# Expert layers of a four-stage transformer stack: routing tables and token map moved into the last shared-expert tiles, first routed block written apart

## The reference, cut to what matters

```python
scores = jax.nn.sigmoid(x @ gate_w.T) + bias
topk_w, topk_idx = jax.lax.top_k(scores, TOPK)          # TOPK = 4 of E = 16 experts
topk_w = topk_w / (jnp.sum(topk_w, axis=-1, keepdims=True) + 1e-20)
cw = jnp.sum(jax.nn.one_hot(topk_idx, E, dtype=x.dtype) * topk_w[..., None], axis=1)
g = jnp.einsum('th,eih->eti', x, Wg)
u = jnp.einsum('th,eih->eti', x, Wu)
z = jax.nn.silu(g) * u
zw = z * cw.T[:, :, None]
out = jnp.einsum('eti,ehi->th', zw, Wd)
out = out + jax.nn.silu(x @ Sg.T) * (x @ Su.T) @ Sd.T   # the shared expert
```

## Time and profile before

| | |
|---|---|
| median of 3 runs | 1276.3 us (1275.05 to 1277.97) |
| the profiled execution | 1276.3 us, span 1274.5 us |
| expert layer 1, first stage ends, routed blocks start | about 71 us, 84 us of the span |
| expert layer 2, the same | about 786 us, 797 us of the span |
| TensorE, VectorE, ScalarE, GpSimd busy | 86%, 71%, 55%, 44% of the span |
| mean granted TensorE clock | 0.924 of 2.4 GHz |

### The profile page before, as it was taken

The page is one execution under the profiler, slowest core; times in us unless marked ns, Lnnn a source line. Parts: engine busy times, 40 slices in busy tenths (PEclk is TensorE's granted clock), DMA queues, the critical chain, the costliest instruction groups (busy, mean ns, idle before and its releaser), DMA issues. The chain is left out here.

```text
span 1274.5 us, 21579 instructions
## 1 busy us (share of the span) xinstructions
PE 1097.4 (86%) x5654; PEld 717.9 (56%) x5655; DVE 905.9 (71%) x1775; ACT 704.8 (55%) x1218; POOL 566.7 (44%) x582
## 2 busy tenths in 40 slices
PE   4969999999194899999997787999999947878597
PEld 3847777777182233333333675677777735467454
DVE  5869888887575888888860666888888847444632
ACT  3238787887143177777775131787888824424142
POOL 4335666664556244443331225566666545140200
PEclk9979999999596599999998888999999977989889
DMA  9367899764615550000000183789995561000001
GB/s 351 114 220 185 218 243 286 174 114 60 192 50 155 104 99 19 1 1 1 1 1 1 63 309 111 236 196 258 275 222 103 83 156 67 1 1 1 0 1 66
DMA packets 62798, 151.01 MB, mean 118 GB/s; under 512 B 12224, under 2 KB 17024, under 8 KB 58240
## 3 DMA queue, kind: packets, MB, share of 16 engines
q1 hardware_dynamic: 37440, 95.17, 22.3%
q0 software_dynamic: 22592, 50.27, 20.3%
q10 hardware_dynamic: 2688, 4.65, 1.1%
HBM read 104.89 MB, written 44.97 MB: 118 GB/s over the span
## 5 line engine op out<-in xcount | busy, mean ns | idle before, releaser
L811 POOL DMA_INDIRECT moe_acc_rows<-xn,moe_token_of x94 | 208.0, 2213 | 146.3 <-ACT xn L886 131.1
L923 DVE TENSOR_TENSOR moe_w_lo<-moe_raw,moe_w_hi 128x1536 fp32r<-128x1536 f32 x94 | 165.4, 1759 | 62.9 <-ACT moe_w_hi L874 62.7
L1977 ACT ACTIVATE causal_prob<-causal_sc 128x512 f32<-128x512 f32 (+3 forms) x384 | 166.8, 492 | 70.3 <-PE causal_sc L1882 69.7
L874 ACT CAST moe_w_hi<-moe_raw 128x1536 fp32r x94 | 138.7, 1475 | 78.0 <-issue 76.4
L1864 PE MATMUL causal_mx<-ks,causal_qs 96*128 (+4 forms) x384 | 131.4, 353 | 23.0 <-DMA causal_qs<-causal_parts 16.5
L831 PE MATMUL moe_gu<-moe_w_hi,xt_hi 128*128 128x512 f32 x282 | 148.4, 526 | 0.6 <-DVE moe_w_lo L923 0.6
L1882 PE MATMUL causal_sc<-causal_qs,ks 99*128 (+3 forms) x384 | 120.2, 333 | 1.9 <-ACT causal_prob L1977 1.7
L831 PE MATMUL moe_gu<-moe_w_hi,xt_lo 128*128 128x512 f32 x282 | 111.8, 396 | 0.0
L831 PE MATMUL moe_gu<-moe_w_lo,xt_hi 128*128 128x512 f32 x282 | 110.9, 393 | 0.0
L826 PE MATMUL moe_gu<-moe_raw,xn 128*128 x188 | 98.0, 603 | 5.0 <-ACT moe_w_hi L874 5.0
L1808 POOL TENSOR_SCALAR_AFFINE_SELECT causal_prob<-causal_prob 128x512 f32<-128x512 f32 x64 | 40.9, 639 | 115.9 <-ACT causal_prob L1977 115.5
(11 more groups left out here) (317 smaller groups left out, 2724.5 us busy)
## 6 DMA issues: line engine op xcount, KB each, us to landing
moe_raw<-in_w_gu SPq DMA_DIRECT2D x34, 1024.0 KB, 6.1
moe_raw<-in_w_down SPq DMA_DIRECT2D x34, 512.0 KB, 8.2
causal_qs<-causal_parts SPq DMA_DIRECT2D x45, 128.0 KB, 3.6
moe_acc_rows<-moe_zeros SPq DMA_DIRECT2D x2, 2304.0 KB, 14.7
moe_acc_rows<-x SPq DMA_DIRECT2D x18, 256.0 KB, 2.0
moe_xn_rows<-xn SPq DMA_DIRECT2D x2, 2048.0 KB, 10.7
x<-moe_acc_rows SPq DMA_DIRECT2D x16, 256.0 KB, 6.8
xn<-moe_acc_rows ACTq DMA_DIRECT2D x16, 256.0 KB, 7.2
```

Source lines behind the costliest of these rows:

```text
L811: pool.indirect_dma_start(acc_rows[a], bass.IndirectOffsetOnAxis(ap=token_of[:, b - 3:b - 2].bitcast(U32), axis=0), out_rows[(b - 3) % OUT ...
L874: nc.scalar.copy(w_hi[1 - s][:, :, :], raw[:, bass.ds(at + SPLIT_AT, GU_COLS - SPLIT_AT)].rearrange("p (k n) -> p k n", k=SPLIT)).then_inc ...
L923: nc.vector.tensor_tensor(w_lo[1 - s][:, :, :], raw[:, bass.ds(at + SPLIT_AT, GU_COLS - SPLIT_AT)].rearrange("p (k n) -> p k n", k=SPLIT), ...
L1977: nc.scalar.activation(prob[u % 2][:, h, o:CH], sc[(u * QPK + h) % BANKS][:, o:CH], ACT.Exp, scale=SCALE).then_inc(exp_done, 1)
```

## The change

First stage. `place()` moves on TensorE from after `down(6)` to before `turn_z(6)`, right behind `gate_up(7)`. GpSimd marks two tiles instead of three (POOL_TILES = 2) and `mark_places` six instead of five. On VectorE `tables()` is cut in three: `begin_tables` (first_of, begun, expert_f) after `add(4)`; `map_tokens` after `z_of(7)`; `place_experts` (expert_of, begun_at) after `zt_lo_of(6)`; `end_tables` (raw_f, raw_at) after `zt_lo_of(7)`. At the end of the first Block TensorE, ScalarE and VectorE wait for the three tables and load the registers of block 0 (`opening`).

Second stage. ScalarE and VectorE skip the steps with b < 0 and run `open_blocks()` instead: the weights of block 0 are split slice by slice (128x512), with the turning of block 0's tokens after the first slice and that of block 1's after the last; the down weights come last. TensorE's block 0 starts when its tokens are turned and the first slice's high part is there, and waits for each slice's low part apart. `hi_gu` and `lo_gu` therefore count two more from then on.

```diff
-            POOL_TILES = 3
+            POOL_TILES = 2
...
+                    if t == T - 1:
+                        place()
                     if 1 <= t <= T:
                         turn_z(t - 1, (t - 1) % 2)
...
-                    if t == T:
-                        place()
+                pe.wait_ge(table_done, 3)
+                opening["pe"] = load_at(pe, 0)
...
+                act.wait_ge(table_done, 3)
+                opening["act"] = act.value_load(expert_of[0:1, 0:1], min_val=1, max_val=E), load_at(act, 0)
...
+                def begin_tables():
+
+                    nc.vector.tensor_copy(first_of[:, :], first[0:1, :]).then_inc(table_done, 1)
+                    nc.vector.tensor_tensor(begun[:, :, :], first[0:1, :].unsqueeze(1).broadcast_to([1, NB, E]),
+                                            row[0:1, 0:NB].unsqueeze(2).broadcast_to([1, NB, E]), ALU.is_le).then_inc(route, 1)
+                    dve.wait_ge(route, 18)
+                    nc.vector.tensor_reduce(expert_f[:, :], begun[:, :, :], AX.X, ALU.add).then_inc(route, 1)
...
+                def place_experts():
+                    nc.vector.tensor_copy(expert_of[:, :], expert_f[:, :]).then_inc(table_done, 1)
                     nc.vector.tensor_tensor(begun_at[:, :, :], begun[:, :, :], raw_step.unsqueeze(1).broadcast_to([1, NB, E]),
                                             ALU.mult).then_inc(route, 1)
...
-                routing = {0: compare, 1: choose, COUNT_AT: place_tokens, COUNT_AT + 1: mark_blocks, COUNT_AT + 2: mark_places}
+                routing = {0: compare, 1: choose, COUNT_AT: place_tokens, COUNT_AT + 1: mark_blocks, COUNT_AT + 2: mark_places,
+                           T - 2: begin_tables}
                 for t in range(T + 2):
                     if t < T:
                         z_of(t, t % 2)
+                    if t == T - 1:
+                        map_tokens()
                     if 1 <= t <= T:
                         zt_lo_of(t - 1, (t - 1) % 2)
+                    if t == T - 1:
+                        place_experts()
+                    if t == T:
+                        end_tables()
                     if t >= 2:
                         add(t - 2, t % 2)
                     if t in routing:
                         routing[t]()
-                    if t == T:
-                        map_tokens()
-                tables()
+                dve.wait_ge(table_done, 3)
+                opening["dve"] = load_at(dve, 0)
...
-                    at = pe.value_load(raw_at[0:1, bass.ds(b, 1)], min_val=0, max_val=(RAW - 1) * W_COLS)
+                    opens = isinstance(b, int) and b == 0
+                    at = opening["pe"] if opens else pe.value_load(raw_at[0:1, bass.ds(b, 1)], min_val=0, max_val=(RAW - 1) * W_COLS)
                     pe.wait_ge(tx_plain, b + 1)
                     pe.wait_ge(tx_lo, b + 1)
-                    pe.wait_ge(hi_gu, b + 1)
+                    pe.wait_ge(hi_gu, 1 if opens else b + SPLIT)
...
-                    pe.wait_ge(lo_gu, b + 1)
+                    if not opens:
+                        pe.wait_ge(lo_gu, b + SPLIT)
                     for k in range(PLAIN, KT):
+                        if opens:
+                            pe.wait_ge(lo_gu, k - PLAIN + 1)
...
+            def open_blocks():
+                expert, at = opening["act"]
+                act.wait_ge(raw_ready, expert)
+                act.sem_inc(act_go, 1)
+                for k in range(SPLIT):
+                    nc.scalar.copy(w_hi[0][:, k, :], raw_slice(at, k)).then_inc(hi_gu, 1)
+                    if k == 0:
+                        turned_hi(-2, -2)
+                turned_hi(-1, -1)
+                nc.scalar.copy(down_hi[0][:, :, :], raw_down(at)).then_inc(hi_down, 1)
...
+            def open_blocks():
+                at = opening["dve"]
+                for k in range(SPLIT):
+                    dve.wait_ge(hi_gu, k + 1)
+                    nc.vector.tensor_tensor(w_lo[0][:, k, :], raw_slice(at, k), w_hi[0][:, k, :].bitcast(F32), ALU.subtract).then_inc(lo_gu, 1)
+                    if k == 0:
+                        turned_lo(-2, -2)
+                turned_lo(-1, -1)
+                dve.wait_ge(hi_down, 1)
+                nc.vector.tensor_tensor(down_lo[0][:, :, :], raw_down(at), down_hi[0][:, :, :].bitcast(F32), ALU.subtract).then_inc(lo_down, 1)
```

More of the change, by code:

```diff
@@ L347, in moe_layer, with load_at @@
             xn_half = m.xn[:, OUTS:T, :].rearrange("p t h -> p (t h)")
+            opening = {}
+            def load_at(eng, b):
+                return eng.value_load(raw_at[0:1, b:b + 1], min_val=0, max_val=(RAW - 1) * W_COLS)
             block = part.enter_context(nc.Block())
@@ L673, in _ @@
                         routing[t]()
[L674 to L676 removed]
+                dve.wait_ge(table_done, 3)
+                opening["dve"] = load_at(dve, 0)
         routed_blocks(m, name, sem, xn_rows, acc_rows, raw, raw_in, load_raw, down_w,
[L679 removed]
+                      silu, z, zt_hi, zt_lo, token_of, expert_of, raw_at, first_of, gathered, rows_out, opening)
 def routed_blocks(m, name, sem, xn_rows, acc_rows, raw, raw_in, load_raw, down_w,
[L683 removed]
+                  silu, z, zt_hi, zt_lo, token_of, expert_of, raw_at, first_of, gathered, rows_out, opening):
     nc = m.nc
@@ L861, in _, with raw_slice, raw_down, turned_hi @@
             run(pe, step)
+        def raw_slice(at, k):
+            return raw[:, bass.ds(at + SPLIT_AT + k * 2 * FI, 2 * FI)]
+        def raw_down(at):
+            return raw[:, bass.ds(at + GU_COLS, W_COLS - GU_COLS)].rearrange("p (i h) -> p i h", i=IT)
         @block.scalar
         def _(act):
+            def turned_hi(b, c):
+                s = c % 2
+                act.wait_ge(tx_done, b + 3)
+                if some(b + 1):
+                    act.wait_ge(gu_done, b + 1)
+                ks, tokens = halves(s)
+                nc.scalar.copy(m.xt_hi[:, ks, tokens], tx[s][:, PLAIN * P:KT * P].rearrange("p (k c) -> p k c", k=SPLIT)).then_inc(tx_hi, 1)
+            def open_blocks():
[8 more added lines that the diff above has]
+                nc.scalar.copy(down_hi[0][:, :, :], raw_down(at)).then_inc(hi_down, 1)
             def step(b, c):
                 s = c % 2
+                if isinstance(b, int) and b < 0:
+                    return
                 if there(b + 1):
@@ L892, in step @@
                 if there(b + 2):
-                    act.wait_ge(tx_done, b + 3)
-                    if some(b + 1):
-                        act.wait_ge(gu_done, b + 1)
-                    ks, tokens = halves(s)
-                    nc.scalar.copy(m.xt_hi[:, ks, tokens], tx[s][:, PLAIN * P:KT * P].rearrange("p (k c) -> p k c", k=SPLIT)).then_inc(tx_hi, 1)
+                    turned_hi(b, c)
                 if there(b - 1):
@@ L915, in _, with turned_lo @@
         def _(dve):
+            def turned_lo(b, c):
+                s = c % 2
+                ks, tokens = halves(s)
+                dve.wait_ge(tx_hi, b + 3)
+                nc.vector.tensor_copy(xt_plain[s][:, :, :], tx[s][:, 0:PLAIN * P].rearrange("p (k c) -> p k c", k=PLAIN)).then_inc(tx_plain, 1)
+                nc.vector.tensor_tensor(m.xt_lo[:, ks, tokens], tx[s][:, PLAIN * P:KT * P].rearrange("p (k c) -> p k c", k=SPLIT),
+                                        m.xt_hi[:, ks, tokens].bitcast(F32), ALU.subtract).then_inc(tx_lo, 1)
+            def open_blocks():
[8 more added lines that the diff above has]
+                nc.vector.tensor_tensor(down_lo[0][:, :, :], raw_down(at), down_hi[0][:, :, :].bitcast(F32), ALU.subtract).then_inc(lo_down, 1)
             def step(b, c):
                 s = c % 2
+                if isinstance(b, int) and b < 0:
+                    return
                 if there(b):
@@ L934, in step @@
                 if there(b + 2):
-                    ks, tokens = halves(s)
-                    dve.wait_ge(tx_hi, b + 3)
-                    nc.vector.tensor_copy(xt_plain[s][:, :, :], tx[s][:, 0:PLAIN * P].rearrange("p (k c) -> p k c", k=PLAIN)).then_inc(tx_plain, 1)
-                    nc.vector.tensor_tensor(m.xt_lo[:, ks, tokens], tx[s][:, PLAIN * P:KT * P].rearrange("p (k c) -> p k c", k=SPLIT),
-                                            m.xt_hi[:, ks, tokens].bitcast(F32), ALU.subtract).then_inc(tx_lo, 1)
+                    turned_lo(b, c)
                 if there(b - 1):
```

23 lines of the change are left out of this document (7 added, 16 removed).

## The result

The changed kernel takes 1268.21 us in the median (1267.12 to 1269.32, 5 runs), the kernel before 1275.37 beside it: ratio 0.9941, 95% interval 0.9928 to 0.9955, or 7.2 us faster. The profiled execution took 1267.42 us with a span of 1265.6, against 1276.3 and 1274.5. The forecast was 1267.9.

The account below looks back on a forecast made before the run. TensorE bounds the routed blocks, so shortening the idle hole ahead of them pays: 4.55 us in layer 1 plus 3.9 in layer 2, 8.45 off 1276.3, gives 1267.9 us; range 1263.8 to 1272.0.

Parts of the forecast that it names:

- the first half: Hole before block 0, up to TensorE's restart: earlier `token_of` moves the restart as much, 5.6 us over both layers.
- the opening: Restart to block 0's first product: slice-by-slice weight split shortens it to 2.7 us, gaining 2.0 and 1.45 us.
- the clock: Block 0 starts at 1.2 GHz: loss of 0.3 us a layer taken, bounded between -1.0 and +1.2.
- Token map: First stage: earlier `place()` gets `token_of` ready 2.85 us sooner in layer 1 and 2.75 in layer 2.
- The condition of the marks: GpSimd's eighth mark is done near 64.6, 0.4 us before `place()`; with twelve marks it would be 67.
- The barrier's owner: End of the first Block: GpSimd's DRAIN ends with the third gather's landing; TensorE restarts 0.3 us behind it.
- rival B: Barrier doesn't move with `token_of`, 1273.4 us; or it moves but block 0's new start gains nothing, 1271.3; 10% for both.
- Where the DRAIN goes from 78.7 to 75.9: First barrier, layer 1: GpSimd's DRAIN ends earlier by the full 2.85 us; other engines have over 2 us of slack.
- Tables at nothing: VectorE's tail: moving four microseconds of tables gains nothing; unmoved they end at 75.85, under a DRAIN ending at 75.9.
- A: Rival: VectorE's work holds GpSimd's gathers, costing up to 1.5 us a layer, 1270.9 us; chance 10%.
- C: Rival: no measurable effect, both gains failing, for instance by missing marks and slice stalls; 1276.3 within 2.5 us; chance 6%.
- D: Rival: slower, TensorE overtakes the gathers of blocks 3 to 7; 1278.3 us if they land 7 us later; chance 6%.

Follow-up runs that it names:

- `POOL_TILES` experiment: Changed kernel with three GpSimd tiles (twelve marks) as before instead of two: 1274.49 us, ratio 0.9989.
- two-gather kernels: Changed kernel with two gathers instead of three in the first stage: 1264.76 us; also with the last x stores moved to the second stage: 1263.91 us.
- the stores' experiment: Changed kernel with the stores of x tiles 5 to 7 and the padding row moved behind the second stage's first weight loads: 1268.09 us, ratio 0.9943.
- the repetition: Changed kernel run again without an edit: 1268.69 us, ratio 0.9944 to the kernel before.
- the halves alone: Kernel before with only the new first stage: 1275.04 us, ratio 0.9992; with only the new block 0 and early register loads: 1274.0 us, ratio 0.9991.
- The kernels kept busy: Unread TensorE products and transposes added around the barrier: kernel before 1272.85 us, kernel before with only the new first stage 1271.94, changed kernel 1267.98.
- the opening alone: Kernel before with only the slice-by-slice block 0 and its registers loaded at the first stage's end: 1274.0 us, ratio 0.9991.
- the first half kept busy: Kernel before with only the new first stage, plus 24 products and 28 transposes that nothing reads on TensorE: 1271.94 us, ratio 0.9963.
- the best kernel: Changed kernel with two gathers in the first stage and the last x stores moved to the second: 1263.91 us; with unread TensorE work added, 1264.84 us.
- changed kernel with padding: Changed kernel plus 22 products and 8 transposes that nothing reads on TensorE around the barrier: 1267.98 us, ratio 0.9938.
- tables at the tail: Changed kernel with all tables put back behind VectorE's last add in one piece, token map still early: 1270.32 us, ratio 0.9954.

## Why the prediction was right, and where it wasn't

The time (1268.21 for 1267.9) and the mechanism were right; that the two lie only 0.3 us apart is luck. Of the 8.45 us of the sum, the traces show 7.3: the first half gave 3.4 in place of 5.6, the opening 3.4 as worked out, and the clock gave 0.5 where 0.6 were to be lost. The sum was taken from 1276.3, while the median of the kernel before is 1275.37 here. The start of layer 2's block 0 (788.68 for 788.7) also owes 0.9 us to stages ahead of the change. Point by point:

1. **Token map: right.** 2.85 and 2.75 us were worked out; 2.94 and 2.82 came. The condition of the marks held: GpSimd's eighth mark ended at 63.59 (59.55 + 4.04 for the last two), 0.2 us before `place()` began at 63.82. With twelve the wait was the 2.07 us of the `POOL_TILES` experiment, as foreseen ("some 1.5 to 2 us behind gate_up(7)"), but the price was 5.8 us in place of 2.6 to 3.6. To block 3 that trace has 6.5 us more than the changed kernel's: 4.8 up to `token_of`, where the forecast of that edit had 2.6 to 3.6 (0.9 of it is `place()` at the lower clock in layer 1), 0.9 from there to the restart and 0.7 in block 0 to block 1.

2. **The barrier's owner: right.** In the traces of before and after GpSimd's DRAIN ends 0.16 to 0.18 us behind the last landing ahead of it (after: 75.88 and 76.06; 785.65 and 785.81), in the two-gather kernels 0.12 to 0.14, and taking a gather away moves it. TensorE restarts 0.28 us behind its end in all of them. The half of rival B in which the barrier stays is out, and the other half by point 5.

3. **The step that failed: "Where the DRAIN goes from 78.7 to 75.9".** The interval from `token_of` to the third landing was taken as fixed, 8.2 us. It grew by 1.23 / 1.13, because the gathers went down among the last stores of x. The text looked at who issues those stores and when they are through, and priced their delay at nothing; it did not ask what else they share. The term of the first half is thus 1.7 us a layer and not 2.85 and 2.75. The Trainium skill (DMA: Bandwidth & Descriptors, "Issuing engines are not separate DMA queues") says that transfers of different engines interleave on the same 16 DMA engines; the stores' experiment agrees, with 1.8 / 1.3 us of landing time given back.

4. **Tables at nothing: right only for the kernel as it is.** The cover was weighed as tables against DRAIN (75.85 against 75.9). It left out that the register loads now stand behind the last table on three engines, some 1.0 us on VectorE and 1.4 on ScalarE. With them the unmoved tables were last in layer 1. The part is worth 1.6 to 2.1 us by the medians, but the trace doesn't show the loads as the price: layer 1's restart was no later for them, and the loss lies in the clock's interval of layer 1 and in the landing of layer 2.

5. **Opening: right.** 2.0 and 1.45 against 1.85 and 1.56. No slice stalled. Block 2 shows a wait of 0.29 us for `w_lo`, one of the signs of being wrong, but the kernel before has the same one, 0.31 us, which the text didn't list:

```profile
94.04 0.50 PE L831 MATMUL moe_gu<-moe_w_hi,xt_hi 128*128 128x512 f32 x1 [0.31 <-DVE moe_w_lo L923]
```

6. **Clock: within its bounds, on the other side of zero.** +0.3 us a layer was taken; block 0 to block 1 changed by -0.45 / -0.05 (-0.09 / -0.01 in the repetition). The bound of -1.0 to +1.2 held. In the halves alone this interval grew by 0.6 to 0.7 us in three layers of four, and a sum of the halves' own medians would have forecast some 2.5 us for this change.

7. **Rivals.** A (gathers held by VectorE, 1270.9): the first and the third gather took 1.42 + 0.95 = 2.37 us, against 2.68. The landing's delay looks the same in the sum, but moving stores and no VectorE work removed it. C is out by the time. D: the gathers of L820 land 4.6, 9.0 (median) and 9.9 us after issue as before, and no idle stands before the transposes of blocks 1 to 3. VectorE did hold GpSimd once in layer 1, with the subtraction for block 1 and not with a slice: one gather took 2.52 us where it took 1.56.

```profile
80.69 0.95 POOL L820 DMA_INDIRECT ks<-moe_xn_rows,moe_token_of  x1 [0.30 <-issue]
80.75 1.22 DVE L978 TENSOR_TENSOR xt_lo<-moe_raw,xt_hi 128x1024 fp32r<-128x1024 f32 x1
...
81.88 1.75 DVE L989 TENSOR_TENSOR moe_w_lo<-moe_raw,moe_w_hi 128x1536 fp32r<-128x1536 f32 x1
...
81.94 2.52 POOL L820 DMA_INDIRECT moe_rows<-moe_xn_rows,moe_token_of  x1 [0.30 <-issue]
```

It starts beside VectorE's subtraction of 1.75 us and cost nothing here. By the Trainium skill (SBUF — State Buffer, "SBUF: two separate sides") the loser is blocked for the whole instruction, but a VectorE instruction with two SBUF inputs blocks only a GpSimd one that reads SBUF. A hold of 1.6 us over the 0.94 alone fits a full block better than the row of before did. The gather at 80.69, which took 0.95 us beside a subtraction of 1.22 with two SBUF inputs, shows no hold at all. In layer 2 three gathers of the changed kernel took 1.31 to 1.59 us, and one of the kernel before 2.28. What decides isn't shown.

**What stays open.** In the traces the two halves with the clock free give 4.7 us and the whole 7.3, and block 0 to block 1, the clock's interval, holds 2.4 of the 2.6 between. The medians of the halves alone give 0.8 and 1.8 us, less than their profiled executions, which were the fastest of the eleven of each. Part of the 7.2 us of the whole is therefore seen in traces of single executions and not in the times of each half. The kernels kept busy confirm the share of the opening on top of the first half in the times as well, but not the first half's.

Some of the mismatch between traces and times lies outside the expert layers' starts. From block 3 to the last block all fourteen traces take the same, 213.6 us in layer 1 and 213.2 (once 213.3) in layer 2. The stages behind, which no edit touches, don't: from layer 1's last block to layer 2's marks row they take 462.2 to 465.6 us, from layer 2's last block to the end 247.0 to 252.3, with a granted clock of 0.89 in the shortest of these and 0.86 in the longest:

```profile
1022.70:1269.70 247.00, 185.70 (x922) 123.72 (x921) 118.34 (x200) 81.24 (x117) 54.12 (x64) 0.89 0.13 37
```
```profile
1018.70:1271.00 252.30, 191.43 (x922) 127.49 (x920) 118.34 (x200) 81.30 (x117) 54.04 (x64) 0.86 0.13 36
```

These are the opening alone and the first half kept busy: the same TensorE instructions take 5.7 us more in the second. Of the 4.8 us by which the profiled execution of the opening alone beat that of the kernel before, 2.5 lie in this last stretch. The mean granted clock of each execution points the same way: four of the eleven of each half were at 0.922, none of them under its kernel's median time, while none of the 27 of the kernel before beside them was under 0.924. Whether an edit moves the clock of the later stages, or they vary by themselves, isn't shown.

## What to carry to other kernels

A Block that ends with indirect DMAs in flight ends with their landing: issue before the barrier only the gathers that the next stage needs first (one less brought the restart 2.3 and 1.8 us forward here). Stores in flight beside them delay the landing; moving them brought the restart forward too, but hardly the time. When a chain is moved earlier, ask what it now lands among, and whose register loads hang on its last result. Behind an idle stretch of TensorE an earlier start pays in full only if the clock's rise comes earlier too, so measure such edits together, and judge each by its own interval in the trace: the total also holds stages that the edit doesn't touch, and here they differed by up to 5 us from trace to trace.

## What was new about the hardware

- After the idle stretch at the barrier (7.7 us before, 6.0 after), TensorE worked at 1.2 GHz from block 0's first product for between 2.9 and 5.9 us, depending on the kernel and the layer, all with the same work in block 0. With the new opening, block 0 to block 1 is 3.47 us at 2.4 GHz throughout; it lay between 4.88 and 6.25 in the kernels that let TensorE idle.
- Keeping TensorE busy across the barrier took 3.1 to 3.4 us off the medians of the two slower kernels, and next to nothing off the two fastest, whose profiled executions did get 1.9 to 3.9 us shorter. It spread the runs: the best kernel's six lie within 1.5 us, with padding within 7.7. The longer executions have the lower mean granted clock (in the changed kernel with padding 1263.17 us at 0.938 and 1270.43 at 0.931), though the clock was held across the barrier in every one that was profiled. Why it falls elsewhere isn't known.
- After 2.07 us of waiting ahead of `place()` its products ran at 1.2 GHz in layer 1 (0.51 over 3.5 us, 2.72 us instead of 1.78); after 2.13 us in layer 2 of the same execution they ran at 2.4 (1.77 us). The length of the wait alone doesn't tell which.
- In layer 1 an engine that loads one register from the tables is through 1.0 us behind the last table, ScalarE with two 1.4 (traces of the tables at the tail and of the opening alone); in layer 2 it is 0.7 and 1.2.
